# A second buffer for the rank rows of the gated layer, and an earlier place for one split

## The chip, the cores and the metric

The kernel runs on one core of a Trainium2 chip. The metric is the device time of one launch in microseconds (us), as the median of several runs. Five engines work side by side, each through its own list of instructions in order: TensorE (PE, matmuls), ScalarE (ACT), VectorE (DVE), GpSimd (POOL) and SyncE (SP), which here issues nearly all transfers. They meet by semaphores: an instruction adds to one when it is done, another engine waits until the count is reached. SBUF is the on-chip memory of 128 partitions; PSUM is the matmul output, eight banks of 128x512 floats.

## The reference

The input x is 8 batches of 128 tokens by 512. Four layers follow, each added to x: a matmul with an adapter's weight (layer 0), a dense layer with gated low-rank experts (layer 1), a dense layer with bias and low-rank part (layer 2), and the gated layer with low-rank parts (layer 3):

```
gate = x @ W_gate.T + SCALE * (x @ A_gate[id].T) @ B_gate[id].T
up   = x @ W_up.T   + SCALE * (x @ A_up[id].T)   @ B_up[id].T
act  = silu(gate) * up                      # 1376 columns, here 11 chunks of 128
x    = x + act @ W_down.T + SCALE * (act @ A_down[id].T) @ B_down[id].T
```

Each batch has its own adapter id. The change lies in the gate and up part of layer 3. B_gate and B_up, the "rank rows", are 16 rows for each batch and chunk.

## The kernel before

The product with W_gate and W_up is made in 11 steps (`STEPS`). Steps 2p and 2p+1 are pair p: two chunks of the 1376 columns, step 2p for gate and 2p+1 for up; the last step (n = 10) takes the one odd chunk with gate and up in it. In a step the two chunks, the two halves of the 512 inputs and the two halves of the tokens form a 2x2 block product, done with seven half-size products in place of eight (Winograd's scheme). So a step has seven `product` calls on PE (L1342, six matmuls each at L1347 to L1349): p1, p2, then `lora_w` (L1370), p5, p6, p3, `lora_y`, p7, p4, `lora_z_x` (L1418). The `lora` calls (L1329) add the low-rank parts, two matmuls for each of four blocks. Steps alternate between PSUM banks 0 to 3 and 4 to 7.

Every float32 operand of a matmul is split in two parts of fewer bits. For a weight tile this is a copy on ACT ("high") and a subtraction on DVE ("low"):

- `wc_high(n, part)` L618 and `wc_low(n, part)` L967 split the weights of step n in three parts: 0 (the blocks of p1 and p2), 1 (the four sums S1 to S4 that POOL forms in `form_s(n)`, L506) and 2 (the block of p4). p1(n) waits for the first, p5(n) for the second, p4(n) for the third. `form_s(n)` waits for `wc_low(n-1, 1)`, since s_tmp has one buffer.
- `bgu_high(n, i)` L629 and `bgu_low(n, i)` L972 split the rank rows of step n, chunk i (128x512). `lora_w(n)` waits for i = 0, `lora_z_x(n)` for i = 1. `bgu_high(n, i)` waits for the rows to have landed and for `c22_ready`, that is for `lora_z_x(n-2)` to be done with the place it writes.

The partial sums go from PSUM to `part` by `copy_part(n, k)` on ACT (L673, k = 0 to 3, after p1, p5, p6, p7); PE's p6 waits for k = 0, p3 for k = 1, p7 for k = 2, and the second half of `lora_z_x` for k = 3. `add_c(n, k)` on DVE (L1033) adds the bank to it after the `lora` call k. For a gate step `silu(p, k)` on ACT (L681) waits for `add_c(2p, k)`; `act_product(p, k)` on DVE (L1041) multiplies it with the up step's sum into `act_f`, which holds chunk fc in 4 KB per partition from 24 KB of the region `act` on. For n >= 2 the orders of ACT and DVE are a loop (L740, L1108) that interleaves the splits for step n+1 with the copies and sums of step n; `silu(p, 0)` and `silu(p, 1)` stand just ahead of `copy_part(2p, 3)`, and `bgu_high(n+1, i)` behind it. Steps 0 and 1 and the splits for step 2 are written out by hand.

Transfers are issued by SP in one list. `load_bgu(p)` (L432) brings the rank rows of pair p (eight transfers of 128 KB, one per batch) into the one buffer `bgu_raw`. It may write only when the rows of the pair before are split:

```
for p in range(1, PAIRS + 1):
    sp.wait_ge(bgu_ready, bgu_count(2 * p - 1, 1))
    load_bgu(p)
    if p < PAIRS:
        sp.wait_ge(wc_lo, 3 * 2 * p)
        for fc in F_ORDER[2 * p + 2:2 * p + 4]:
            load_wgu(fc)
```

`load_wgu` brings the weights of one chunk (512 KB), for the pair after the next. The last semaphore named in the change, `main_done`, counts the output tiles of layers 1 and 2; at 16 all of layer 2's matmuls are done, and with them the last readers of what lay at 44 to 52 KB of `act`.

Of the kernel before, what the change touches and what calls it, by code (L numbers as in the profile page):

```python
# [35 lines left out]
P = 128  # L36
B, S, D = 8, 128, 512
# [20 lines left out]
STEPS = 2 * PAIRS + 1  # L58
# [3 lines left out]
def bass_four_residual_layers(nc, xT, ids0, ids1, ids2, ids3, w0, w1, aw1, b1, w2, a2, b2, bias2,  # L62
                              wgu, agu, sel, bgu, wd, ad, bd, out):
    ctx = ExitStack()
    with ctx:
# [14 lines left out]
        o_slot2 = o_raw + 16 * KB  # L80
# [33 lines left out]
        t3_sb = at("t3_sb", o_w0, [H, S])  # L114
        t3_sel = at("t3_sel", o_act + 68 * KB, [2, 2, P])
        t3_st = at("t3_st", o_tp, [2, T], F32R)
        bgu_raw = at("bgu_raw", o_slot2, [2, B // 2, 2, P])
        bgu_st = [at(f"bgu_st{i}", o_bst + i * 4 * KB, [B // 2, 2, P], F32R) for i in range(2)]
        wgu_raw = [at(f"wgu_raw{i}", o_raw + i * 4 * KB, [C, 2, P]) for i in range(4)]
        xt = [at(f"xt{i}", o_xa + i * 8 * KB, [2, 2, HT], F32R) for i in range(3)]  # L120
# [56 lines left out]
        def sem(name):  # L177
            return ctx.enter_context(nc.semaphore(name))
# [7 lines left out]
        w2_in, a2_in, b2_in, bias_in = sem("w2_in"), sem("a2_in"), sem("b2_in"), sem("bias_in")  # L186
        agu_in, sel_in = sem("agu_in"), sem("sel_in")
        wgu_in = [sem(f"wgu_in{i}") for i in range(4)]
        bgu_in = sem("bgu_in")
        ad_in, bd_in = sem("ad_in"), sem("bd_in")  # L190
        wd_in = [sem(f"wd_in{o}") for o in range(C)]
        out_sent = sem("out_sent")
# [135 lines left out]
        def wgu_block(n, i, first, end):  # L328

            fc, g = rows_of(n)[i]  # L330
            return wgu_raw[raw_slot(fc)][:, first:end, g]

        def bgu_views(n, i):

            raw = bgu_raw[:, 0, :, i] if n == STEPS - 1 else bgu_raw[:, i, :, n % 2]
            return raw, bgu_st[1 - i][:, :, n % 2]

        def bgu_count(n, i):
# [41 lines left out]
        def _(sp):  # L380
# [50 lines left out]

            def load_bgu(p):  # L432

                for b in range(B):
                    rows = slice(64 * (b % 2), 64 * (b % 2) + 64)
                    if p < PAIRS:
                        f1 = 2 * p + 1
                        sp.dma_start(bgu_raw[rows, :, b // 2],  # L438
                                     bgu[adapter3[b], f1:f1 + 2].rearrange("f r n -> r f n")).then_inc(bgu_in, 16)
                    else:  # L440
                        sp.dma_start(bgu_raw[rows, 0, b // 2], bgu[adapter3[b], 0]).then_inc(bgu_in, 16)

            sp.wait_ge(w12_lo, nth["w2_3"])
            load_wgu(1)
# [4 lines left out]
            sp.wait_ge(l2_tm, 2)  # L449
            for b in range(B):  # L450
                sp.dma_start(ad_raw[:, b], ad[adapter3[b]]).then_inc(ad_in, 16)
            for p in range(1, PAIRS + 1):
                sp.wait_ge(bgu_ready, bgu_count(2 * p - 1, 1))
                load_bgu(p)
                if p < PAIRS:
                    sp.wait_ge(wc_lo, 3 * 2 * p)
                    for fc in F_ORDER[2 * p + 2:2 * p + 4]:
                        load_wgu(fc)
# [71 lines left out]
        def _(act):  # L530
# [87 lines left out]
            def wc_high(n, part_of):  # L618
                src, hi, _ = wc_views(n, part_of)
                if part_of == 0:  # L620
                    if n >= 2:
                        act.wait_ge(c21_ready, n - 1)
                    for fc, _ in rows_of(n):
                        act.wait_ge(wgu_in[raw_slot(fc)], 16 * raw_uses(fc))
                elif part_of == 1:
                    act.wait_ge(s_formed, 4 * (n + 1))
                high(hi, src).then_inc(wc_hi, 1)

            def bgu_high(n, i):  # L629
                raw, st = bgu_views(n, i)  # L630
                act.wait_ge(bgu_in, 16 * B * (n // 2 + 1))
                if n >= 2:
                    act.wait_ge(c22_ready, n - 1)
                elif i == 1:
                    act.wait_ge(main_done, 16)
                high(st, raw).then_inc(bgu_hi, 1)
# [36 lines left out]
            def copy_part(n, k):  # L673

                done, b = ((p1_done, 0), (p5_done, 2), (p6_done, 0), (p7_done, 0))[k]
                act.wait_ge(done, n + 1)
                if n >= 2:
                    act.wait_ge(silu_done if n % 2 == 0 else act_mul, 4 * (n // 2))
                high(part[n % 2][k][:], bank[4 * (n % 2) + b][:]).then_inc(part_copied[n % 2], 1)
# [49 lines left out]
            for k in (0, 1):  # L729
                silu(0, k)  # L730
            wc_high(2, 0)
            copy_part(1, 3)
            for k in (2, 3):
                silu(0, k)
            for part_of in (1, 2):
                wc_high(2, part_of)
            for i in range(2):
                bgu_high(2, i)

            for n in range(2, STEPS):  # L740
                p, g = divmod(n, 2)
# [45 lines left out]
        def _(dve):  # L787
# [253 lines left out]
            def act_product(p, k):  # L1041
                i, h = c_place(k)
                dst = act_f[:, rows_of(2 * p)[i][0], h * HT:(h + 1) * HT]
                dve.wait_ge(silu_done, 4 * p + k + 1)
                dve.wait_ge(c_added, 8 * p + 4 + k + 1)
                dve.tensor_tensor(dst, part[1][C_PART[k]][:], dst, ALU.mult).then_inc(act_mul, 1)
# [51 lines left out]
            wc_low(2, 0)  # L1098
            add_c(1, 0)
            act_product(0, 0)  # L1100
            for part_of in (1, 2):
                wc_low(2, part_of)
            add_c(1, 1)
            act_product(0, 1)
            for i in range(2):
                bgu_low(2, i)

            for n in range(2, STEPS):  # L1108
                p, g = divmod(n, 2)
# [496 lines left out]
```

## Time and profile before

| | |
|---|---|
| median of 3 runs | 301.67 us (300.73 to 302.11) |
| the profiled execution, its own time | 303.5 us |
| its span, first to last instruction | 301.7 us |
| mean granted TensorE clock | 0.987 of full |
| busy: PE, DVE, ACT, POOL | 291.2, 197.8, 143.8, 45.9 us |
| chain that ended last, by engine | PE 80%, DVE 7%, DMA 5%, ACT 3% |

The span is what lies between the first and the last instruction of the trace; the execution's own time holds 1.8 us more around it. All times of rows below are in microseconds from the span's start. A timeline row gives the start of the first instruction of a group, the time from there to the end of the last, and in brackets how long the engine sat idle before it and who released it. Consecutive matmuls overlap: the distance of two starts is what one costs.

### The profile page before, as it was taken

The page shows a single profiled execution, that of the slowest core. Times are in us where ns is not written, and L with a number is a line of the kernel's source. Part 1 is how long each engine was busy: PE and PEld are TensorE (multiplying, and loading weights), DVE is VectorE, ACT ScalarE, POOL GpSimd, SP SyncE. Part 2 cuts the span into 40 slices and gives each one's busy share as a digit, 9 for nine tenths or more (in the row PEclk, how much of TensorE's full clock was granted, in tenths as well). Part 3 has the DMA queues.
Part 4 walks back from the last instruction along what each step waited for, and adds up shares of the span by engine and source line. Part 5 has one row for each costly group of instructions (what it writes and reads, how often), then busy time and mean ns, then how long its engine had stood idle before and what let it go on. Part 6 is the DMA issues. An engine that isn't in the chain of part 4 may idle for free.

```text
span 301.7 us, 4571 instructions
## 1 busy us (share of the span) xinstructions
PE 291.2 (96%) x1624; PEld 239.0 (79%) x1624; DVE 197.8 (66%) x343; ACT 143.8 (48%) x255; POOL 45.9 (15%) x67
## 2 busy tenths in 40 slices
PE   6999999999999999959999999999999999999995
PEld 5457788988888788847888888888889888888884
DVE  1288897985567999776686786776656959242003
ACT  2378672503335297834646636656634874211000
POOL 1000000001706207043053043123000000000000
PEclk9999999999999999987999999999999999999999
DMA  4999863008403000250250350420275200022005
GB/s 153 351 393 395 323 236 107 0 4 259 156 0 99 0 3 0 88 193 0 79 199 2 107 174 0 128 84 8 63 276 180 73 0 0 0 72 70 0 2 139
DMA packets 23255, 33.29 MB, mean 110 GB/s; under 512 B 2624, under 2 KB 15424, under 8 KB 23104
## 3 DMA queue, kind: packets, MB, share of 16 engines
q1 hardware_dynamic: 22944, 32.47, 32.2%
q10 hardware_dynamic: 288, 0.52, 0.5%
q8 instruction: 13, 0.21, 0.3%
q14 instruction: 10, 0.08, 0.1%
HBM read 30.89 MB, written 2.10 MB: 109 GB/s over the span
## 4 chain that ended last, share of the span: by engine, by line
PE 80%; DVE 7%; DMA 5%; ACT 3%; SPq 2%; issue 2%
PE bank L1224 11%; PE bank L1225 11%; PE bank L1226 11%; PE bank L1347 10%; PE bank L1348 10%; PE bank L1349 10%; DMA w_raw<-in_w 4%; PE bank L1329 3%; PE bank L1179 2%; PE bank L1197 2%; PE bank L1472 2%; SPq L438 2%; DMA bgu_raw<-in_bgu 1%; DVE bgu_st L964 1%; PE bank L1208 1%
## 5 line engine op out<-in xcount | busy, mean ns | idle before, releaser
L533 ACT ACTIVATE part<-bank 128x512 f32<-128x512 f32 x44 | 26.2, 595 | 33.0 <-PE bank L1349 33.0
L1224 PE MATMUL bank<-act_hl,wd_hl 128*128 128x512 f32 (+1 forms) x99 | 36.5, 369 | 0.0
L1225 PE MATMUL bank<-act_hl,wd_hl 128*128 128x512 f32 (+1 forms) x99 | 36.3, 367 | 0.0
L1226 PE MATMUL bank<-act_hl,wd_hl 128*128 128x512 f32 (+1 forms) x99 | 36.2, 366 | 0.0
L1039 DVE TENSOR_TENSOR part<-bank,part 128x512 f32<-128x512 f32 x44 | 29.1, 682 | 6.8 <-PE bank L1329 6.8
L964 DVE SCALAR_TENSOR_TENSOR bgu_st<-bgu_st,lo_rows,bgu_raw 128x512 fp32r<-128x512 f32 x22 | 17.8, 845 | 12.6 <-ACT bgu_st L533 12.5
L790 DVE TENSOR_TENSOR w_hl<-w_raw,w_hl 128x512 fp32r<-128x512 f32 x29 | 19.0, 686 | 9.0 <-ACT w_hl L533 9.0
L533 ACT ACTIVATE act_hl<-act_f 128x512 fp32r<-128x512 f32 x22 | 13.6, 625 | 20.8 <-PE bank L1226 18.8
L790 DVE TENSOR_TENSOR act_hl<-act_f,act_hl 128x512 fp32r<-128x512 f32 x22 | 14.9, 689 | 12.9 <-ACT act_hl L533 12.8
L533 ACT ACTIVATE w_hl<-w_raw 128x512 fp32r<-128x512 f32 x29 | 17.7, 624 | 9.0 <-DMA w_raw<-in_w 8.6
L515 POOL TENSOR_TENSOR s_tmp<-wgu_raw 128x256 f32<-128x256 f32 x11 | 8.4, 760 | 86.8 <-DVE wc_up L790 42.8
L1226 PEld LDWEIGHTS bank<-act_hl,wd_hl 128*128 128x128 f32 x99 | 18.6, 188 | 3.1
L1224 PEld LDWEIGHTS bank<-act_hl,wd_hl 128*128 128x128 f32 x99 | 18.7, 189 | 3.0 <-issue 0.2
L1225 PEld LDWEIGHTS bank<-act_hl,wd_hl 128*128 128x128 f32 x99 | 18.7, 189 | 2.7
L1329 PEld LDWEIGHTS bank<-t_st,bgu_st 128*128 128x128 f32 x88 | 14.8, 191 | 6.4 <-DVE bgu_st L964 3.7
L1347 PE MATMUL bank<-xb,wc_gate 128*128 128x512 f32 x48 | 19.6, 409 | 0.0
L1329 PE MATMUL bank<-t_st,bgu_st 128*128 128x256 f32 x88 | 16.2, 289 | 3.3 <-DVE bgu_st L964 3.3
L1349 PE MATMUL bank<-xb,wc_gate 128*128 128x512 f32 x48 | 19.4, 403 | 0.0
L1348 PE MATMUL bank<-xb,wc_gate 128*128 128x512 f32 x48 | 19.3, 403 | 0.0
L685 ACT ACTIVATE act_f<-part 128x512 f32<-128x512 f32 x22 | 13.6, 630 | 10.8 <-DVE part L1039 10.8
L1081 DVE TENSOR_TENSOR x_f<-bank,x_f 128x512 f32<-128x512 f32 (+1 forms) x9 | 5.5, 629 | 19.5 <-PE bank L1493 19.5
L1347 PE MATMUL bank<-xb,wc_up 128*128 128x512 f32 x40 | 15.8, 395 | 0.0
(162 smaller groups left out, 702.5 us busy)
## 6 DMA issues: line engine op xcount, KB each, us to landing
w_raw<-in_w SPq DMA_DIRECT2D x22, 256.0 KB, 7.6
wgu_raw<-in_wgu SPq DMA_DIRECT2D x11, 512.0 KB, 4.4
bgu_raw<-in_bgu SPq DMA_DIRECT2D x40, 128.0 KB, 2.7
w_raw<-in_w SPq DMA_DIRECT2D x7, 512.0 KB, 7.4
wd_raw<-in_wd SPq DMA_DIRECT2D x4, 704.0 KB, 6.1
out<-x_f SPq DMA_DIRECT2D x7, 256.0 KB, 2.4
x_f<-in_xT SPq DMA_DIRECT2D x6, 256.0 KB, 8.2
w_raw<-in_w SPq DMA_DIRECT2D x1, 1024.0 KB, 5.7
```

What stands on the lines that cost most here:

```text
L533: return act.activation(dst, src, ACT.Copy)
L685: act.activation(act_f[:, fc, h * HT:(h + 1) * HT], part[0][C_PART[k]][:], ACT.Silu).then_inc(silu_done, 1)
L790: return dve.tensor_tensor(dst, src, hi.bitcast(F32), ALU.subtract)
L964: return dve.scalar_tensor_tensor(out=st, in0=st.bitcast(F32), scalar=lo_rows16[:, 0:1], in1=raw, op0=ALU.mult, op1=ALU.add)
L1039: dve.tensor_tensor(dst[:], bank[4 * (n % 2) + b][:], dst[:], ALU.add).then_inc(c_added, 1)
L1224: pe.matmul(dst, w_hi, x[0][:, cols], start=start, stop=False)
L1225: pe.matmul(dst, w_hi, x[1][:, cols], start=False, stop=False)
L1226: return pe.matmul(dst, w_lo, x[0][:, cols], start=False, stop=stop)
L1329: ins = pe.matmul(dst[:, q * 2 * S:(q + 1) * 2 * S], bgu_views(n, i)[1][:, pair], t3_st[:, g, pair * 2 * S:(pair + 1) * 2 * S], start=Fals ...
L1347: pe.matmul(dst[:], hi, x[0][c], start=(start and c == 0), stop=False, skip_group_check=True)
L1348: pe.matmul(dst[:], hi, x[1][c], start=False, stop=False, skip_group_check=True)
L1349: ins = pe.matmul(dst[:], lo, x[0][c], start=False, stop=(stop and c == 1), skip_group_check=True)
```

## The change

The rank rows of pair 1 (steps 2 and 3) get a buffer and a semaphore of their own, at 44 to 52 KB of `act`, where `act_f` keeps chunks 5 and 6, first written in step 4. All other pairs use the old buffer. SP issues the load of pair 1 once `main_done` has reached 16, right behind the loads of `ad`; in the loop it still waits for `bgu_ready` at p = 1, but then goes on to the weights. The splits of step 2's rank rows move: on ACT `bgu_high(2, i)` from behind `wc_high(2, 2)` to behind `wc_high(2, 0)`, and on DVE `bgu_low(2, i)` from behind `act_product(0, 1)` to ahead of `wc_low(2, 1)`.

```
--- before.py
+++ after.py
@@ -114,7 +114,7 @@
         t3_sb = at("t3_sb", o_w0, [H, S])
         t3_sel = at("t3_sel", o_act + 68 * KB, [2, 2, P])
         t3_st = at("t3_st", o_tp, [2, T], F32R)
-        bgu_raw = at("bgu_raw", o_slot2, [2, B // 2, 2, P])
+        bgu_raw = [at(f"bgu_raw{i}", off, [2, B // 2, 2, P]) for i, off in enumerate([o_slot2, o_act + 44 * KB])]
         bgu_st = [at(f"bgu_st{i}", o_bst + i * 4 * KB, [B // 2, 2, P], F32R) for i in range(2)]
         wgu_raw = [at(f"wgu_raw{i}", o_raw + i * 4 * KB, [C, 2, P]) for i in range(4)]
         xt = [at(f"xt{i}", o_xa + i * 8 * KB, [2, 2, HT], F32R) for i in range(3)]
@@ -186,7 +186,7 @@
         w2_in, a2_in, b2_in, bias_in = sem("w2_in"), sem("a2_in"), sem("b2_in"), sem("bias_in")
         agu_in, sel_in = sem("agu_in"), sem("sel_in")
         wgu_in = [sem(f"wgu_in{i}") for i in range(4)]
-        bgu_in = sem("bgu_in")
+        bgu_in = [sem(f"bgu_in{i}") for i in range(2)]
         ad_in, bd_in = sem("ad_in"), sem("bd_in")
         wd_in = [sem(f"wd_in{o}") for o in range(C)]
         out_sent = sem("out_sent")
@@ -330,9 +330,18 @@
             fc, g = rows_of(n)[i]
             return wgu_raw[raw_slot(fc)][:, first:end, g]
 
+        def bgu_place(p):
+
+            return 1 if p == 1 else 0
+
+        def bgu_landed(p):
+
+            return 16 * B * (p if p > 1 else 1)
+
         def bgu_views(n, i):
 
-            raw = bgu_raw[:, 0, :, i] if n == STEPS - 1 else bgu_raw[:, i, :, n % 2]
+            raw = bgu_raw[bgu_place(n // 2)]
+            raw = raw[:, 0, :, i] if n == STEPS - 1 else raw[:, i, :, n % 2]
             return raw, bgu_st[1 - i][:, :, n % 2]
 
         def bgu_count(n, i):
@@ -431,14 +440,15 @@
 
             def load_bgu(p):
 
+                raw, landed = bgu_raw[bgu_place(p)], bgu_in[bgu_place(p)]
                 for b in range(B):
                     rows = slice(64 * (b % 2), 64 * (b % 2) + 64)
                     if p < PAIRS:
                         f1 = 2 * p + 1
-                        sp.dma_start(bgu_raw[rows, :, b // 2],
-                                     bgu[adapter3[b], f1:f1 + 2].rearrange("f r n -> r f n")).then_inc(bgu_in, 16)
+                        sp.dma_start(raw[rows, :, b // 2],
+                                     bgu[adapter3[b], f1:f1 + 2].rearrange("f r n -> r f n")).then_inc(landed, 16)
                     else:
-                        sp.dma_start(bgu_raw[rows, 0, b // 2], bgu[adapter3[b], 0]).then_inc(bgu_in, 16)
+                        sp.dma_start(raw[rows, 0, b // 2], bgu[adapter3[b], 0]).then_inc(landed, 16)
 
             sp.wait_ge(w12_lo, nth["w2_3"])
             load_wgu(1)
@@ -449,9 +459,12 @@
             sp.wait_ge(l2_tm, 2)
             for b in range(B):
                 sp.dma_start(ad_raw[:, b], ad[adapter3[b]]).then_inc(ad_in, 16)
+            sp.wait_ge(main_done, 16)
+            load_bgu(1)
             for p in range(1, PAIRS + 1):
                 sp.wait_ge(bgu_ready, bgu_count(2 * p - 1, 1))
-                load_bgu(p)
+                if p > 1:
+                    load_bgu(p)
                 if p < PAIRS:
                     sp.wait_ge(wc_lo, 3 * 2 * p)
                     for fc in F_ORDER[2 * p + 2:2 * p + 4]:
@@ -628,7 +641,7 @@
 
             def bgu_high(n, i):
                 raw, st = bgu_views(n, i)
-                act.wait_ge(bgu_in, 16 * B * (n // 2 + 1))
+                act.wait_ge(bgu_in[bgu_place(n // 2)], bgu_landed(n // 2))
                 if n >= 2:
                     act.wait_ge(c22_ready, n - 1)
                 elif i == 1:
@@ -729,13 +742,13 @@
             for k in (0, 1):
                 silu(0, k)
             wc_high(2, 0)
+            for i in range(2):
+                bgu_high(2, i)
             copy_part(1, 3)
             for k in (2, 3):
                 silu(0, k)
             for part_of in (1, 2):
                 wc_high(2, part_of)
-            for i in range(2):
-                bgu_high(2, i)
 
             for n in range(2, STEPS):
                 p, g = divmod(n, 2)
@@ -1098,12 +1111,12 @@
             wc_low(2, 0)
             add_c(1, 0)
             act_product(0, 0)
+            for i in range(2):
+                bgu_low(2, i)
             for part_of in (1, 2):
                 wc_low(2, part_of)
             add_c(1, 1)
             act_product(0, 1)
-            for i in range(2):
-                bgu_low(2, i)
 
             for n in range(2, STEPS):
                 p, g = divmod(n, 2)
```

## Rows read from the trace of the kernel before

**Rows 1.** Waits of the matmul engine (PE) over the whole span: total, times, longest, in us.

```profile
PE bank L1329 <- DVE bgu_st L964: 3.3, 1, 3.3
```

**Rows 2.** Timeline of PE: start us, us, engine, line, tiles, form, count, [idle before <-releaser].

```profile
6.76 5.56 PE L1197 MATMUL bank<-w_raw,x_f 128*128 128x512 f32 x8 [1.02 <-DMA w_raw<-in_w]
...
127.89 0.39 PE L1347 MATMUL bank<-xb,wc_gate 128*128 128x512 f32 x1
...
130.41 0.40 PE L1349 MATMUL bank<-xb,wc_gate 128*128 128x512 f32 x1
134.08 0.80 PE L1329 MATMUL bank<-t_st,bgu_st 128*128 128x256 f32 x2 [3.28 <-DVE bgu_st L964]
...
144.90 0.40 PE L1347 MATMUL bank<-xb,wc_up 128*128 128x512 f32 x1
...
155.43 0.39 PE L1347 MATMUL bank<-xb,wc_gate 128*128 128x512 f32 x1
```

**Rows 3.** Busy time by window: us, busy per engine (instructions), granted clock, DMA share, GB/s.

```profile
3.00:12.40 9.40, 8.38 (x22) 4.76 (x22) 0.56 (x1) 0.77 (x2) 0.00 (x0) 1.00 0.80 258
102.40:113.00 10.60, 10.60 (x105) 8.54 (x105) 9.69 (x13) 8.00 (x17) 0.00 (x0) 1.00 0.01 2
130.60:134.10 3.50, 0.22 (x2) 0.02 (x1) 1.95 (x3) 1.49 (x3) 2.47 (x3) 0.91 0.77 287
134.10:140.20 6.10, 6.10 (x15) 4.87 (x16) 5.34 (x8) 2.37 (x5) 0.00 (x0) 0.50 0.02 6
144.90:155.60 10.70, 10.70 (x53) 9.00 (x52) 7.97 (x12) 6.37 (x12) 3.09 (x4) 1.00 0.51 167
```

**Rows 4.** Timeline of SyncE's DMA queue, 90 to 160 us.

```profile
90.53 4.32 SPq L451 DMA_DIRECT2D ad_raw<-in_ad  x8
122.81 6.13 SPq L438 DMA_DIRECT2D bgu_raw<-in_bgu  x8
128.98 1.07 SPq L430 DMA_DIRECT2D wgu_raw<-in_wgu  x2
145.98 6.07 SPq L438 DMA_DIRECT2D bgu_raw<-in_bgu  x8
```

**Rows 5.** Timeline of ScalarE (ACT), 90 to 160 us.

```profile
123.81 0.62 ACT L533 ACTIVATE wc_gate<-wgu_raw 128x512 fp32r<-128x512 f32 x1
125.76 0.60 ACT L533 ACTIVATE part<-bank 128x512 f32<-128x512 f32 x1 [1.33 <-PE bank L1349]
...
132.61 1.15 ACT L533 ACTIVATE bgu_st<-bgu_raw 128x512 fp32r<-128x512 f32 x2 [3.97 <-DMA bgu_raw<-in_bgu]
...
143.25 0.60 ACT L533 ACTIVATE part<-bank 128x512 f32<-128x512 f32 x1
...
148.10 0.58 ACT L533 ACTIVATE part<-bank 128x512 f32<-128x512 f32 x1
...
154.35 1.15 ACT L533 ACTIVATE bgu_st<-bgu_raw 128x512 fp32r<-128x512 f32 x2
```

**Rows 6.** Timeline of VectorE (DVE), 90 to 160 us.

```profile
126.79 0.69 DVE L1046 TENSOR_TENSOR act_f<-part,act_f 128x512 f32<-128x512 f32 x1
128.38 1.23 DVE L790 TENSOR_TENSOR wc_gate<-s_tmp,wc_gate 128x1024 fp32r<-128x1024 f32 x1 [0.89 <-ACT wc_gate L533]
...
129.85 0.68 DVE L1039 TENSOR_TENSOR part<-bank,part 128x512 f32<-128x512 f32 x1
130.64 1.12 DVE L1046 TENSOR_TENSOR act_f<-part,act_f 128x512 f32<-128x512 f32 x1
133.28 1.42 DVE L964 SCALAR_TENSOR_TENSOR bgu_st<-bgu_st,lo_rows,bgu_raw 128x512 fp32r<-128x512 f32 x2 [1.51 <-ACT bgu_st L533]
134.61 1.28 DVE L1039 TENSOR_TENSOR part<-bank,part 128x512 f32<-128x512 f32 x2
...
137.61 0.68 DVE L1039 TENSOR_TENSOR part<-bank,part 128x512 f32<-128x512 f32 x1
```

**Rows 7.** Timeline of GpSimd (POOL), 90 to 150 us.

```profile
129.77 0.77 POOL L515 TENSOR_TENSOR s_tmp<-wgu_raw 128x256 f32<-128x256 f32 x1 [8.92 <-DVE wc_gate L790]
```

More of the change, by code:

```diff
@@ L116, in bass_four_residual_layers @@
         t3_st = at("t3_st", o_tp, [2, T], F32R)
-        bgu_raw = at("bgu_raw", o_slot2, [2, B // 2, 2, P])
+        bgu_raw = [at(f"bgu_raw{i}", off, [2, B // 2, 2, P]) for i, off in enumerate([o_slot2, o_act + 44 * KB])]
         bgu_st = [at(f"bgu_st{i}", o_bst + i * 4 * KB, [B // 2, 2, P], F32R) for i in range(2)]
@@ L188, in bass_four_residual_layers @@
         wgu_in = [sem(f"wgu_in{i}") for i in range(4)]
-        bgu_in = sem("bgu_in")
+        bgu_in = [sem(f"bgu_in{i}") for i in range(2)]
         ad_in, bd_in = sem("ad_in"), sem("bd_in")
@@ L331, in wgu_block, with bgu_place, bgu_landed @@
             return wgu_raw[raw_slot(fc)][:, first:end, g]
+        def bgu_place(p):
+            return 1 if p == 1 else 0
+        def bgu_landed(p):
+            return 16 * B * (p if p > 1 else 1)
         def bgu_views(n, i):
-            raw = bgu_raw[:, 0, :, i] if n == STEPS - 1 else bgu_raw[:, i, :, n % 2]
+            raw = bgu_raw[bgu_place(n // 2)]
+            raw = raw[:, 0, :, i] if n == STEPS - 1 else raw[:, i, :, n % 2]
             return raw, bgu_st[1 - i][:, :, n % 2]
@@ L432, in load_bgu @@
             def load_bgu(p):
+                raw, landed = bgu_raw[bgu_place(p)], bgu_in[bgu_place(p)]
                 for b in range(B):
@@ L437, in load_bgu @@
                         f1 = 2 * p + 1
-                        sp.dma_start(bgu_raw[rows, :, b // 2],
-                                     bgu[adapter3[b], f1:f1 + 2].rearrange("f r n -> r f n")).then_inc(bgu_in, 16)
+                        sp.dma_start(raw[rows, :, b // 2],
+                                     bgu[adapter3[b], f1:f1 + 2].rearrange("f r n -> r f n")).then_inc(landed, 16)
                     else:
-                        sp.dma_start(bgu_raw[rows, 0, b // 2], bgu[adapter3[b], 0]).then_inc(bgu_in, 16)
+                        sp.dma_start(raw[rows, 0, b // 2], bgu[adapter3[b], 0]).then_inc(landed, 16)
             sp.wait_ge(w12_lo, nth["w2_3"])
@@ L451, in _ @@
                 sp.dma_start(ad_raw[:, b], ad[adapter3[b]]).then_inc(ad_in, 16)
+            sp.wait_ge(main_done, 16)
+            load_bgu(1)
             for p in range(1, PAIRS + 1):
                 sp.wait_ge(bgu_ready, bgu_count(2 * p - 1, 1))
-                load_bgu(p)
+                if p > 1:
+                    load_bgu(p)
                 if p < PAIRS:
@@ L630, in bgu_high @@
                 raw, st = bgu_views(n, i)
-                act.wait_ge(bgu_in, 16 * B * (n // 2 + 1))
+                act.wait_ge(bgu_in[bgu_place(n // 2)], bgu_landed(n // 2))
                 if n >= 2:
@@ L731, in _ @@
             wc_high(2, 0)
+            for i in range(2):
+                bgu_high(2, i)
             copy_part(1, 3)
@@ L736, in _ @@
                 wc_high(2, part_of)
-            for i in range(2):
-                bgu_high(2, i)
             for n in range(2, STEPS):
@@ L1100, in _ @@
             act_product(0, 0)
+            for i in range(2):
+                bgu_low(2, i)
             for part_of in (1, 2):
@@ L1104, in _ @@
             act_product(0, 1)
-            for i in range(2):
-                bgu_low(2, i)
             for n in range(2, STEPS):
```

## The prediction

> **What bounds the kernel now.** I read the waits of PE first, since PE is busy nearly the whole span. They show one wait worth naming after the start: 3.3 us, once, for the split rank rows [rows 1]. The timeline of PE places it: p2 of step 2 issues its last matmul at 130.41, and the next instruction, `lora_w(2)`, starts at 134.08 after 3.28 us of idle [rows 2]. Matmuls go out every 0.23 us (127.89 to 130.41 is 2.52 for 11 of them), so `lora_w(2)` could have started at 130.64: 3.44 us lost. The windows show a second loss: behind the gap, from 134.1 to 140.2, the granted clock is 0.50, the 1.2 GHz level, where the step after has 1.00, 2.4 GHz [rows 3]. PE had stood still before it fell, and worked without a break when it rose.
>
> Both losses are read from step lengths. Step 2 takes 144.90 - 127.89 = 17.01 us, step 3 takes 155.43 - 144.90 = 10.53 [rows 2]. The excess is 6.48 us: 3.44 of gap and 3.04 of half clock. That is the most that removing this wait can bring.
>
> Who makes the wait? ACT sat 3.97 us until the rows had landed at 132.61, split them and let DVE go at 133.28 [rows 5, 6]. SP had issued the eight transfers from 122.81 to 128.94 [rows 4], because their one buffer came free only with the splits of step 1. So the chain is: split of step 1, eight issues, landing, ACT, DVE, PE. In later pairs the same chain starts at the same place but has a whole step to run in, and PE does not wait.
>
> **The load of pair 1.** It moves from 122.81 to the end of layer 2's matmuls, about 102.5. SP's queue is empty then: its transfers before ended at 94.85 [rows 4]. From first issue to ACT's start the load took 132.61 - 122.81 = 9.8 us, so it lands near 112.3. ACT will ask for it at 124.3: 12 us of cover, and the bound of this cost from above is what would be left if the load took twice as long, still nothing. Behind it on SP stands the wait for `bgu_ready` that was there before (it let SP go at 122.81), and behind that two weight loads, which now go out at 122.8 instead of 128.98; their readers are in step 4, after 140, so that earlier place brings nothing. Could the eight transfers disturb work at 102.4 to 113, where PE is busy 10.60 of 10.60 and DVE 9.69 [rows 3]? Nothing shows them there. The nearest row is the window 144.9 to 155.6, with a DMA share of 0.51, clock 1.00 and PE without idle time [rows 3]. I take 0. The far end of the bound: a DVE subtraction or product goes from 0.69 to 1.12 in the worst neighbourhood of the trace, beside POOL [rows 6, 7]; if all of DVE's 9.69 us stretched like that it would cost 6 us. I give it little weight, since DVE's sums last 0.68 both at 129.85, with transfers under way, and at 137.61, with a DMA share of 0.02, and a product with both inputs in SBUF 0.69 at 126.79, beside the transfers [rows 3, 6].
>
> **ACT's order.** The two copies of `bgu_high(2)` (1.15 us) now follow `wc_high(2, 0)`, which starts at 123.81 and lasts 0.62, so they run 124.3 to 125.5. `copy_part(1, 3)` is behind them; it starts at 125.76 when PE lets it, after 1.33 us of idle [rows 5]. The copies fit in that idle: cost 0. Were they 0.5 us longer, `copy_part(1, 3)` would still be ready long before PE needs it at 127.4 or so. Its condition, the end of `lora_z_x(0)`, lies 18 matmuls and eight `lora` matmuls of 0.12 ahead of p1(2), so at 127.89 - 5.1 = 122.8, in time.
>
> **DVE's order.** Here cover is thin. `bgu_low(2)` now starts when `act_product(0, 0)` has issued, at 127.40 (126.79 + 0.6), and takes 134.61 - 133.28 = 1.33 [rows 6]. So `wc_low(2, 1)` starts at 128.73 instead of 128.38 and ends near 129.95. p5(2) asks for it at 130.64 + 0.24 = 130.88: 0.9 us of slack. `lora_w(2)` finds its rows from 128.2 on. The gap at 130.64 goes, and with it the fall of the clock.
>
> What is late next is DVE. Before, it caught up while PE stood and while PE ran at half clock. Now it has this list from 128.73 on, with durations from [rows 6]: `wc_low(2, 1)`, `wc_low(2, 2)` and `add_c(1, 1)` 2.26 (128.38 to 130.64), so to 130.99; `act_product(0, 1)` 1.12 beside POOL, to 132.1; two sums, a split, two products and the sum `add_c(2, 0)`, before from 134.61 to 138.29, of which the next can start at 3.6, to 135.7; `wc_low(3, 1)` and `(3, 2)` 1.47 (128.38 to 129.85), to 137.2; `add_c(2, 1)` 0.68, to 137.85. Then ACT's `silu(1, 1)` 0.63 and `copy_part(2, 3)` 0.60, with 0.04 of handing over each, to 139.15. Only then may the second half of `lora_z_x(2)` go. PE, at full rate from 127.89, is there at 127.89 + 10.53 - 0.24 = 138.2. **So a new wait of 0.9 us** arises at the end of step 2.
>
> It has a small echo. Before, from the start of `copy_part(2, 3)` at 143.25 to the end of `copy_part(3, 0)` at 148.68 it took 5.43 us [rows 5], through the splits, DVE's sums and two silus. From 138.55 on that ends at 144.0. PE wants it for p6(3) at 139.15 + 0.24 + 18 x 0.23 + 0.24 = 143.8: 0.2 us more. After that step 3 stands as before against the other engines.
>
> The load of pair 2 starts when `bgu_low(3)` is done, in which step 3 is now about 0.8 us later against PE. ACT took its rows at 154.35 [rows 5]; from ACT's start to the first split ready it is 133.28 + 0.75 - 132.61 = 1.4 [rows 5, 6], so they were ready near 155.8. `lora_w(4)` needed them 12 matmuls after 155.43, near 158.2. Of 2.4 us of slack about 1.6 are left. Cost 0.
>
> **Sum.** 3.44 + 3.04 - 0.9 - 0.2 = 5.4 us, of which I take 5.3 (a semaphore or two more in a chain of so many steps). The profiled execution has 303.5 us, its span 301.7; it would be 298.2. The median of the runs shown lies 1.8 lower, at 301.67, and I carry the same difference over: **296.4 us**. The bounds of the new waits: none if DVE's product is not stretched and its order closes up; 2 us if every sum and split in the list stretches as the product did for the 3.4 us in which POOL forms its sums. So the case runs from 295.2 to 297.4.
>
> **Rivals.** What this kernel's measurement can tell from no change is 0.5%, 1.5 us.
>
> 1. No new wait at all: 6.48 us gained, 295.2. For it: ACT and DVE are idle in part of each steady step (DVE 7.97 of 10.70, [rows 3]). Against: the list above has no gap in it.
> 2. The new wait brings the clock down once. 0.50 for 6.1 us cost 3.04, so the gain is 5.4 - 3.0 = 2.4 and the time 299.3. For: the clock fell once after an idle time. Against: PE sat idle 1.02 us until 6.76, and the window around it, 3.0 to 12.4, has clock 1.00 [rows 2, 3]. 0.9 is nearer to 1.02 than to 3.28.
> 3. Slower: the clock falls again and again, at the short waits that ends of steps now have while DVE is behind. The place is the end of steps 2, 3, 4; each fall costs 3.0. It decides once 6.48 + 1.5 = 8.0 us are lost, that is 1.1 of waits and 2.3 falls; three falls give 301.67 - 6.48 + 1.1 + 9.1 = 305.4. Against: at half clock PE is slow enough for DVE to catch up (step 2 of before), so one fall ends the cause. The Trainium skill's page "TensorE: Matmul & The Clock Gate", in "A second HAM failure mode: psum-queue depth-cycling", says that short idle times between groups of matmuls, frequent enough, make the clock swing between its two levels. By that rule this rival is what would come; the trace so far has only the 1.02 us at full clock against it.
> 4. The change doesn't bring what it says: pair 1's load is held up beyond 130, or its transfers stretch the stretch from 102 to 113 by the 6 us of the bound above. Then 301.7. Against it stand 12 us of cover and the equal durations beside DMA.
>
> **How the numbers follow.** The forecast gets 0.62, rival 1 0.17, rival 2 0.12, rival 4 0.05, rival 3 0.04. The range runs from 294.8 (rival 1 and half a us for medians of runs that spread over 1.4) to 299.6, which takes in rival 2 and leaves out 3 and 4. Faster is the sum of the first three, 0.91; within 0.5% 0.05; slower 0.04.
>
> **What would show it.** The waits of PE name no `bgu_st` of 3 us. The granted clock stays 1.00 from 115 on, and step 2 takes near 11.4 us from p1 to p1, step 3 near 10.7. Eight transfers of rank rows start near 102.5. A wait below 1 us stands ahead of the last `lora` matmuls of step 2, released by ACT's copy into `part`. I am wrong if the clock falls in steps 2 to 4, if `p5(2)` waits for DVE, or if PE idles between 102 and 122.

## The result, and the profile after

The changed kernel takes 298.67 us (median of 6 runs, 298.31 to 299.24) against 301.63 us for the kernel before (6 runs): ratio 0.9921, interval 0.9897 to 0.9945. That is 0.8% faster, 2.4 us by the ratio (the two medians differ by 3.0 us), where 5.3 us were forecast. The direction and the range held; the size was about twice what came.

The changed kernel was compared once more on another chip, after the first experiments below, with a ratio of 0.990 to 0.993 expected and a mean clock of 0.998 or more in nearly all of its runs; had a part of the gain belonged to the first chip, the ratio would have been nearer to 0.995. It came to 298.98 us against 301.33 us, ratio 0.9921 (0.9892 to 0.9950), with 0.999 or 1.00 in five of six runs and 0.994 in one.

The profiled execution shows a span of 296.7 us and a clock of 1.00. Against the profiled execution of before (301.7) that is 5.0 us less, very near the forecast. So the first question is why the profiles differ by 5.0 us and the runs by less than 3.

The waits of PE after the start, in answer to [rows 1]: the 3.3 us for `bgu_st` are gone, and two short ones for ACT's copies into `part` have come.

```profile
PE bank L1342 <- ACT part L546: 0.7, 1, 0.7
...
PE bank L1360 <- ACT part L546: 0.2, 1, 0.2
```

The timeline of PE, in answer to [rows 2]:

```profile
127.77 0.39 PE L1360 MATMUL bank<-xb,wc_gate 128*128 128x512 f32 x1
...
130.51 0.40 PE L1342 MATMUL bank<-t_st,bgu_st 128*128 128x256 f32 x2
...
139.04 0.51 PE L1342 MATMUL bank<-t_st,bgu_st 128*128 128x256 f32 x2 [0.73 <-ACT part L546]
139.38 0.40 PE L1360 MATMUL bank<-xb,wc_up 128*128 128x512 f32 x1
...
144.16 0.50 PE L1360 MATMUL bank<-xt,wc_up 128*128 128x512 f32 x1 [0.25 <-ACT part L546]
...
150.47 0.39 PE L1360 MATMUL bank<-xb,wc_gate 128*128 128x512 f32 x1
```

`lora_w(2)` follows p2 at once, at 130.51. Step 2 lasts 139.38 - 127.77 = 11.61 us, step 3 lasts 150.47 - 139.38 = 11.09. The wait at the end of step 2 and its echo at p6(3) stand where the forecast put them, with 0.73 and 0.25 us for 0.9 and 0.2.

Three windows, in answer to [rows 3] (columns as there). The clock is 1.00 in all of them. In the first, with the rank rows now coming in, DVE is busy 9.84 us and was 9.69, and PE has no idle time:

```profile
102.40:113.00 10.60, 10.60 (x105) 8.53 (x99) 9.84 (x13) 8.01 (x17) 0.00 (x0) 1.00 0.33 101
...
127.00:139.00 12.00, 11.31 (x54) 9.27 (x53) 10.73 (x16) 6.86 (x13) 5.27 (x7) 1.00 0.01 1
139.00:150.00 11.00, 10.71 (x49) 8.63 (x50) 7.86 (x11) 6.54 (x12) 3.81 (x6) 1.00 0.42 124
```

SyncE's queue, in answer to [rows 4]: the load of pair 1 starts at 102.50, the weights at 122.51, pair 2's rows at 141.41.

```profile
102.50 6.13 SPq L448 DMA_DIRECT2D bgu_raw<-in_bgu  x8
122.51 0.82 SPq L439 DMA_DIRECT2D wgu_raw<-in_wgu  x2
141.41 6.08 SPq L448 DMA_DIRECT2D bgu_raw<-in_bgu  x8
```

ACT, in answer to [rows 5]: the two copies of rank rows run at 124.18, `copy_part(1, 3)` still has 0.32 us of idle ahead of it. `wc_high(3, 1)` waits 0.51 for POOL; `silu(1, 1)` and `copy_part(2, 3)` are the end of the chain that holds PE.

```profile
124.18 1.14 ACT L546 ACTIVATE bgu_st<-bgu_raw 128x512 fp32r<-128x512 f32 x2
125.63 0.60 ACT L546 ACTIVATE part<-bank 128x512 f32<-128x512 f32 x1 [0.32 <-PE bank L1362]
...
133.45 1.06 ACT L546 ACTIVATE wc_up<-s_tmp 128x1024 fp32r<-128x1024 f32 x1 [0.51 <-POOL s_tmp L533]
...
137.87 0.63 ACT L698 ACTIVATE act_f<-part 128x512 f32<-128x512 f32 x1 [1.44 <-DVE part L1052]
138.41 0.58 ACT L546 ACTIVATE part<-bank 128x512 f32<-128x512 f32 x1
```

DVE, in answer to [rows 6]: from 127.27 to 137.84 (137.16 + 0.68) it is never idle. The product beside POOL takes 1.13 and the split at 133.12 takes 0.85 instead of 0.68.

```profile
127.27 1.41 DVE L977 SCALAR_TENSOR_TENSOR bgu_st<-bgu_st,lo_rows,bgu_raw 128x512 fp32r<-128x512 f32 x2
128.60 1.22 DVE L803 TENSOR_TENSOR wc_gate<-s_tmp,wc_gate 128x1024 fp32r<-128x1024 f32 x1
...
130.86 1.13 DVE L1059 TENSOR_TENSOR act_f<-part,act_f 128x512 f32<-128x512 f32 x1
...
133.12 0.85 DVE L803 TENSOR_TENSOR wc_up<-wgu_raw,wc_up 128x512 fp32r<-128x512 f32 x1
133.89 1.28 DVE L1059 TENSOR_TENSOR act_f<-part,act_f 128x512 f32<-128x512 f32 x2
...
137.16 0.68 DVE L1052 TENSOR_TENSOR part<-bank,part 128x512 f32<-128x512 f32 x1
139.54 1.70 DVE L977 SCALAR_TENSOR_TENSOR bgu_st<-bgu_st,lo_rows,bgu_raw 128x512 fp32r<-128x512 f32 x2 [1.71 <-ACT bgu_st L546]
```

### The profile page after: what moved, and what is told of

Read it like the earlier page. It is cut to its first block, busy times and chain, and to the rows that moved or that the text cites. A ratio compares the mean times of both kernels' runs of the same rounds, so it can differ in the third digit from the quotient of the medians.

```text
span 296.7 us, 4572 instructions
## 1 busy us (share of the span) xinstructions
PE 286.5 (97%) x1624; PEld 235.8 (79%) x1624; DVE 197.0 (66%) x343; ACT 143.8 (48%) x255; POOL 45.3 (15%) x67
## 4 chain that ended last, share of the span: by engine, by line
PE 86%; DVE 5%; DMA 4%; issue 2%; ACT 1%; SPq 1%; DVEq 0%; ACTq 0%
PE bank L1237 12%; PE bank L1238 12%; PE bank L1239 12%; PE bank L1360 10%; PE bank L1361 10%; PE bank L1362 10%; DMA w_raw<-in_w 4%; PE bank L1342 3%; PE bank L1192 2%; PE bank L1485 2%; PE bank L1221 1%; PE bank L1284 1%; PE bank L1174 1%; PE bank L1222 1%; PE bank L1223 1%
## 5 line engine op out<-in xcount | busy, mean ns | idle before, releaser
L1360 PE MATMUL bank<-xb,wc_gate 128*128 128x512 f32 x48 | 18.9, 394 | 0.0
L1362 PE MATMUL bank<-xb,wc_gate 128*128 128x512 f32 x48 | 18.9, 394 | 0.0
L1361 PE MATMUL bank<-xb,wc_gate 128*128 128x512 f32 x48 | 18.8, 392 | 0.0
```

Of the source, the lines that this page charges most:

```text
L1360: pe.matmul(dst[:], hi, x[0][c], start=(start and c == 0), stop=False, skip_group_check=True)
L1361: pe.matmul(dst[:], hi, x[1][c], start=False, stop=False, skip_group_check=True)
L1362: ins = pe.matmul(dst[:], lo, x[0][c], start=False, stop=(stop and c == 1), skip_group_check=True)
```

## Why the runs gained less than the profiles: the kernel before, again

These runs take the kernel before again, and then the two halves of the change by themselves.

**The unchanged kernel.** No edit.

> The unchanged kernel once more, for the spread of its own runs. Theory T1: the term of the forecast that was mis-sized is the half clock behind the gap. The profiled execution of before took 303.5 us with 3.04 us lost to the clock; the median run takes 301.6, 1.9 less, so most runs should lose only about 1.1 us to the clock, and their mean granted clock should lie above 0.987, near 0.993 to 0.996. Rival T2: the clock loses 3 us in every run and the 1.9 us lie in the loads at the start, which differ between executions; then the clocks of all runs are near 0.987 and the spans differ without it. A gap of 3.4 us is there in every profile under both.

Measured: 301.14 us (12 runs), ratio 1.0007. In this profile the span is 299.1 and the clock 1.00. DVE and PE:

```profile
131.12 1.12 DVE L1046 TENSOR_TENSOR act_f<-part,act_f 128x512 f32<-128x512 f32 x1
132.16 2.36 DVE L964 SCALAR_TENSOR_TENSOR bgu_st<-bgu_st,lo_rows,bgu_raw 128x512 fp32r<-128x512 f32 x2
```

```profile
133.43 0.51 PE L1329 MATMUL bank<-t_st,bgu_st 128*128 128x256 f32 x2 [2.15 <-DVE bgu_st L964]
...
146.54 0.50 PE L1347 MATMUL bank<-xt,wc_up 128*128 128x512 f32 x1 [0.29 <-ACT part L533]
```

Here the rows were taken by ACT at 131.41, 8.15 us after the first issue at 123.26, not after 9.8. DVE went from `act_product(0, 1)` to `bgu_low(2)` without idle. So the gap of 2.15 us was set by DVE's list, and the clock did not fall. Two more profiles of the same kernel were taken at the end, on a third chip:

> A third profile of the unchanged kernel, to see the usual execution. If DVE's list sets the gap in most executions, the rows land 8.0 to 8.7 us after the first issue, the gap is 2.1 to 2.3 us, and where the mean clock is below 1.00 its fall stands directly behind the gap, in 131 to 141, and costs 0.5 to 1.5 us. If the first profile was the usual one, the gap is above 3 us again.

> A fourth profile of the unchanged kernel; the same is expected of it as of the third.

In the third profile (301.05 us) the rows are taken after 8.13 us and the gap is 2.16 us, as in the second. But here the clock fell behind the gap, to 0.50 from 133.8 to 137.2, and it took PE 6.05 us from `lora_w(2)` to `lora_y(2)`, where the second profile has 4.46 (133.43 to 137.89):

```profile
132.97 0.50 PE L1329 MATMUL bank<-t_st,bgu_st 128*128 128x256 f32 x2 [2.16 <-DVE bgu_st L964]
...
139.02 0.39 PE L1329 MATMUL bank<-t_st,bgu_st 128*128 128x256 f32 x2
```

The fourth profile (302.78 us) is like the first in the landing: ACT waits 4.00 us for rows that it takes 9.84 us after their first issue at 123.35, and PE's gap is 3.32 us.

```profile
133.19 1.15 ACT L533 ACTIVATE bgu_st<-bgu_raw 128x512 fp32r<-128x512 f32 x2 [4.00 <-DMA bgu_raw<-in_bgu]
```

Expectation and outcome agree for the third and not for the fourth. In both profiles with late rows it is the last of the eight transfers alone that is late: it lands 4.2 and 4.3 us after its issue, where the seven others take 2.6 to 2.9 us, and the last one takes 2.6 us in the second and the third profile.

The four profiles of before, with the time from `lora_w(2)` to `lora_y(2)`, in which the clock is lowered or not, and with the stretch from the last `lora` matmuls of step 1 to those of step 3 (in the first profile 127.42 to 154.96):

| execution | rows taken after | gap | mean clock | `lora_w(2)` to `lora_y(2)` | stretch |
|---|---|---|---|---|---|
| before, the first, on which the forecast rests | 9.80 us | 3.28 us | 0.987 | 7.34 us | 27.54 us |
| the second | 8.15 | 2.15 | 1.00 | 4.46 | 24.48 |
| the third | 8.13 | 2.16 | 0.992 | 6.05 | 25.10 |
| the fourth | 9.84 | 3.32 | 0.994 | 6.05 | 26.30 |
| the changed kernel, two profiles | | 0.73 at the end of step 2 | 1.00 | 4.38 | 22.70 and 22.71 |

What is left of the span outside the stretch is nearly the same in all six, 274.0 to 274.7 us, so the difference of the two kernels lies in the stretch. The first profile has the longest stretch and the lowest clock: its clock is at 0.50 from about 133.5 to about 140.3, for 6.8 us, against 3.4 us in the third and in the fourth (135.4 to 138.8). The fall costs PE 2.9 us in the first (7.34 against 4.46) and 1.6 us in the third and the fourth. Of the 1.6 us only 0.6 show in the stretch at the gap of 2.15 us (25.10 against 24.48). The other 1.0 stands in the second profile as waits of PE for what DVE's list makes late: the last `lora` matmuls of step 2 take 0.4 us more there, and p6(3), with the 0.29 us shown above, loses 0.6. Behind a slow PE both are gone. At the gap of 3.3 us DVE has caught up already and the whole 1.6 us show.

Of 58 runs of before with a recorded clock (12 of them from the repetition above, the others from the comparisons on two chips), 19 have a mean clock of 1.00 and a median time of 300.71 us, 29 lie at 0.992 or 0.994, and 10 below 0.99, from 301.74 to 303.54 us. The profiled execution of 303.5 us belongs to the last. (One more run of before, on the third chip, took 299.72 us at a clock of 0.994.) Only 8 of the 58 took more than 302.4 us, as both profiles with late rows did. A run without a profile shows no landing, so this is an estimate from times: late rows are nearer to one execution in seven than to the one in two of the profiles.

Theory T1 was half right: most runs lose less to the clock. But landing and gap vary as well, which it had denied, and T2, differences in the loads at the start, isn't needed. With the third profile as the usual one (its 301.05 us are near the median of the 58 runs, 301.2) the change is worth 25.10 - 22.70 = 2.4 us, which is what the ratio of 0.9921 says.

**The early load alone.** From the changed kernel, the two moves of splits are undone:

```
             wc_high(2, 0)
-            for i in range(2):
-                bgu_high(2, i)
             copy_part(1, 3)
...
             for part_of in (1, 2):
                 wc_high(2, part_of)
+            for i in range(2):
+                bgu_high(2, i)
...
             act_product(0, 0)
-            for i in range(2):
-                bgu_low(2, i)
...
             act_product(0, 1)
+            for i in range(2):
+                bgu_low(2, i)
```

> Pair 1's rows loaded early to their own place, the splits of step 2 in the order of before. The copies on ACT then run at about 128.6, the two on DVE behind act_product(0, 1) at about 131.7, the first ready near 132.5, where lora_w(2) asks at 130.6: a gap of 1.8 to 2.0 us in place of 3.4. Under T1 and T2 alike the wait is this long. If a gap of 1.9 us keeps the clock at 1.00 then DVE has 1.9 us more to catch up and the wait at the end of step 2 goes: about 0.9 to 1.0 us over the changed kernel, 299.5. If the clock falls as well, up to 3 us more.

Measured: 301.02 us (12 runs), ratio 1.000 (0.9981 to 1.0019). The gap is 2.15 us. ACT has the copies made at 128.96, two microseconds ahead of need:

```profile
128.96 1.14 ACT L546 ACTIVATE bgu_st<-bgu_raw 128x512 fp32r<-128x512 f32 x2
```

but DVE comes to them only behind the product:

```profile
131.05 1.13 DVE L1059 TENSOR_TENSOR act_f<-part,act_f 128x512 f32<-128x512 f32 x1
132.11 2.34 DVE L977 SCALAR_TENSOR_TENSOR bgu_st<-bgu_st,lo_rows,bgu_raw 128x512 fp32r<-128x512 f32 x2
```

The gap is 2.15 us where 1.8 to 2.0 were expected, with the pair of splits at 2.34 us beside POOL. The expected 299.5 us was 1.5 too low: I had let one wait of about 1 us stand for the whole, but the gap, 0.4 us at the last `lora` matmuls of step 2 and an echo of 0.28 us in step 3 all stay, so the stretch is 24.47 us against 22.70; and the clock was lowered in 7 of the 12 runs. What the run shows is that the new buffer alone brings nothing that can be measured, to within 0.6 us. A late landing cost 1.2 us (26.30 against 25.10) and can't reach PE here; had it been there in half of the executions of before, this run should have been about 0.6 us faster, which is the edge of its interval. A second profile:

> A second profile of the early load alone. The landing can't reach PE here, so the gap is 2.1 to 2.2 us again whatever the execution. If the mean clock is below 1.00, the fall stands behind the gap, which would show that a gap of 2.15 us is enough for it in some executions, without any late landing.

The gap is 2.15 us again, and this time the clock fell behind it, with the landing out of the question:

```profile
100.00:130.00 30.00, 30.00 (x201) 24.48 (x200) 26.75 (x35) 21.65 (x39) 6.79 (x7) 1.00 0.21 71
...
133.00:136.00 3.00, 2.24 (x9) 1.90 (x10) 3.00 (x5) 0.00 (x0) 1.22 (x2) 0.84 0.02 5
136.00:139.00 3.00, 3.00 (x10) 2.36 (x9) 3.00 (x6) 1.92 (x3) 0.00 (x0) 0.59 0.00 0
139.00:142.00 3.00, 3.00 (x16) 2.50 (x15) 1.68 (x3) 2.06 (x5) 2.23 (x3) 1.00 0.00 0
```

Between 133 and 139 the granted clock is 0.84 and 0.59, from 100 to 133 and behind 139 it is 1.00. One and the same gap of 2.15 us left the clock alone in the first profile and not in the second. The stretch grew from 24.47 to 25.10 us, 0.6 us for the fall and not 3.0. As in the kernel before, the fall is shorter than the one that I read (1.6 us of PE's time), and while PE is slow, DVE catches up: the echo of 0.28 us and the 0.4 us at the end of step 2 are gone. The mean clock of this profile, 0.987, holds a second fall, from 12 to 16 us, where the granted clock is 0.57; so a mean clock alone does not say where the clock fell.

**The new order alone**, with the load as before (the same moves of ACT and DVE, in the kernel before):

> The splits of step 2 at their new place, the load as before. ACT then waits for rows that land near 132.5 with copy_part(1, 3), two silus and the second part of the weights behind it, so PE waits at lora_z_x(1), at 127.4, for copy_part(1, 3) until about 134.3, and then for p5(2)'s weights. Expected 5 to 8 us slower than before, 306 to 310, with the clock at its lower level behind it. If it is not slower than 303 I have the chain of ACT wrong.

Measured: 305.66 us, ratio 1.0151 (1.0123 to 1.0179). ACT stands 7.06 us until the rows land, with `copy_part(1, 3)` behind it, and PE waits 5.33 us for that copy:

```profile
131.72 1.15 ACT L533 ACTIVATE bgu_st<-bgu_raw 128x512 fp32r<-128x512 f32 x2 [7.06 <-DMA bgu_raw<-in_bgu]
132.77 0.58 ACT L533 ACTIVATE part<-bank 128x512 f32<-128x512 f32 x1
```

```profile
133.40 0.79 PE L1329 MATMUL bank<-t_st,bgu_st 128*128 128x256 f32 x2 [5.33 <-ACT part L533]
```

The chain is as expected, and so is the clock, 0.50 from 130 to 136; the time is 0.3 us below the lower end. The two halves are worth 0.0 and +4.6 us alone and -2.4 together: the order needs the load, and the load shows no gain without the order.

## DVE's list, tested

**Products later.** The changed kernel, DVE's list in step 2:

```
-                if g == 0:
+                if g == 0 and n != 2:
                     for k in (2, 3):
                         act_product(p - 1, k)
...
                 add_c(n, 1)
+                if n == 2:
+                    for k in (2, 3):
+                        act_product(0, k)
```

> The changed kernel with act_product(0, 2) and (0, 3) moved from ahead of add_c(2, 0) to behind add_c(2, 1) on DVE: 1.2 us less ahead of add_c(2, 1). If DVE's list in step 2 is what makes PE wait 0.7 us at the end of step 2 and 0.25 us in step 3, both waits go and the time falls by 0.7 to 1.0 us below the changed kernel, to about 297.8. Rival: it is POOL's sums, 0.2 us later than before, that hold wc_high(3, 1) and all behind it; then the wait stays above 0.4.

Measured: 298.27 us, ratio 0.9908 (0.9885 to 0.9931). The time alone doesn't tell it from the changed kernel (0.9897 to 0.9945); the trace does. The wait at the end of step 2 is gone, though ACT's `wc_high(3, 1)` still waits 0.51 us for POOL, so it was DVE's list and not POOL's sums. But the echo in step 3 grew from 0.25 to 0.76 us:

```profile
143.76 0.50 PE L1363 MATMUL bank<-xt,wc_up 128*128 128x512 f32 x1 [0.76 <-ACT part L546]
```

```profile
136.11 0.68 DVE L1052 TENSOR_TENSOR part<-bank,part 128x512 f32<-128x512 f32 x1
136.71 1.83 DVE L1059 TENSOR_TENSOR act_f<-part,act_f 128x512 f32<-128x512 f32 x2
138.50 2.34 DVE L977 SCALAR_TENSOR_TENSOR bgu_st<-bgu_st,lo_rows,bgu_raw 128x512 fp32r<-128x512 f32 x2
```

The two products moved to 136.71, beside POOL's sums for step 4, and took 1.83 us in place of 1.28; the two splits behind them took 2.34 in place of 1.70. Half of the expected gain was eaten there: the stretch is 22.26 us, 0.44 below the changed kernel.

**Splits ahead of the product.** The early load alone, with one more edit in DVE's list:

```
             add_c(1, 1)
+            for i in range(2):
+                bgu_low(2, i)
             act_product(0, 1)
-            for i in range(2):
-                bgu_low(2, i)
```

> Pair 1's rows early, ACT's order of before, and on DVE bgu_low(2) ahead of act_product(0, 1) instead of behind it. If DVE's list, not the landing, sets the gap of 2.15 us, then it starts about 1.05 us earlier (131.0 instead of 132.1) and the gap is 1.0 to 1.5 us. The rest of DVE's list is as long as before, so up to 0.5 us of it comes back as a wait at the end of step 2. Time 300.2 to 300.7, 0.3 to 0.8 us below the early load alone. If the gap stays at 2.1, POOL's sums beside bgu_low, not the order, hold it.

Measured: 299.68 us (12 runs), ratio 0.9941 (0.9922 to 0.9959), 0.5 us better than the range.

```profile
130.83 0.50 PE L1342 MATMUL bank<-t_st,bgu_st 128*128 128x256 f32 x2 [0.45 <-DVE bgu_st L977]
...
139.93 0.50 PE L1342 MATMUL bank<-t_st,bgu_st 128*128 128x256 f32 x2 [1.24 <-ACT part L546]
...
145.05 0.50 PE L1360 MATMUL bank<-xt,wc_up 128*128 128x512 f32 x1 [0.25 <-ACT part L546]
```

The gap fell from 2.15 to 0.45 us. I had expected 1.0 to 1.5, with the splits held by POOL; but the first split got in between POOL's first and second sum and it was the second sum that stretched, to 1.29 us from 0.72, and the pair took 1.88 us instead of 2.34. 1.24 us came back at the end of step 2. This is the list at work: what is taken from the first wait comes back in part at the next.

The stretch is 23.88 us, 0.59 below the early load alone, within the 0.3 to 0.8 expected. The runs gained more, 1.3 us by the medians and 1.8 by the ratios. A part of that is likely the clock, though no profile shows it: 11 of these 12 runs have a mean clock of 0.997 or more, where the early load alone has 5 of 12 at 1.00.

**DVE's new order without ACT's:**

```
             wc_high(2, 0)
-            for i in range(2):
-                bgu_high(2, i)
             copy_part(1, 3)
...
             for part_of in (1, 2):
                 wc_high(2, part_of)
+            for i in range(2):
+                bgu_high(2, i)
```

> Pair 1's rows early and DVE's new order, but ACT's order of before. bgu_high(2) then runs at 128.9 to 130.1, bgu_low(2) from 129.5 to 130.9, and wc_low(2, 1) behind it to 132.1, so lora_w(2) waits little and p5(2) waits about 1.2 us; DVE's list is 2 us later than in the changed kernel, so the wait at the end of step 2 is 1.5 to 2 us. Time 300.5 to 301.5, no better than before. If it comes to 298.7, ACT's new order is worth nothing and DVE's is all.

Measured: 300.57 us (10 runs), ratio 0.9984 (0.9960 to 1.0009), within the expectation. DVE waits for ACT's copies at 128.50, and everything behind is late. PE has four short waits:

```profile
131.10 0.50 PE L1360 MATMUL bank<-xb,wc_gate 128*128 128x512 f32 x1 [0.77 <-DVE wc_gate L803]
...
136.27 0.50 PE L1360 MATMUL bank<-xt,wc_gate 128*128 128x512 f32 x1 [0.54 <-ACT part L546]
...
140.27 0.50 PE L1342 MATMUL bank<-t_st,bgu_st 128*128 128x256 f32 x2 [0.73 <-ACT part L546]
...
145.40 0.50 PE L1360 MATMUL bank<-xt,wc_up 128*128 128x512 f32 x1 [0.28 <-ACT part L546]
```

The wait at p5(2) is 0.77 instead of 1.2, and at the end of step 2 0.73 instead of 1.5 to 2, since 0.54 of it is spent at p7(2) already. The stretch is 24.52 us, as long as with the early load alone (24.47). So ACT's move carries weight, 1.6 us by the medians on this chip (300.57 against 298.98), though it stood in the forecast at a cost of 0 and no gain. The profiled execution was the fastest of the ten and has a clock of 1.00; four of the ten have 0.993 or 0.994 and took 301.39 to 301.74 us. No profile shows where the clock fell in those.

**Rows early.** The changed kernel with both waits attacked. On ACT `bgu_high(3)` goes ahead of `silu(1, 1)`; on DVE `act_product(0, 2)` and `(0, 3)` go behind `add_c(2, 3)`:

```
                 elif g == 0:
-                    for k in (0, 1):
-                        silu(p, k)
+                    silu(p, 0)
+                    if n == 2:
+                        for i in range(2):
+                            bgu_high(n + 1, i)
+                    silu(p, 1)
                 copy_part(n, 3)
-                if more:
+                if more and n != 2:
...
                 for k in (2, 3):
                     add_c(n - 1, k)
+                if n == 3:
+                    for k in (2, 3):
+                        act_product(0, k)
...
-                if g == 0:
+                if g == 0 and n != 2:
                     for k in (2, 3):
                         act_product(p - 1, k)
```

> The changed kernel with three more moves around step 2: bgu_high(3) on ACT ahead of silu(1, 1), and act_product(0, 2) and (0, 3) on DVE behind add_c(1+1, 2) and (1+1, 3) in the list of step 3 instead of ahead of add_c(2, 0). This takes 1.2 us out of the list ahead of add_c(2, 1) and lets bgu_low(3) start about 1.5 us sooner, so that both short waits of the changed kernel (0.73 and 0.25 us) go. Expected 0.7 to 1.0 us below the changed kernel, about 297.8, with no wait of PE between 100 and 160. Rival: as in the run with the products later alone, one wait goes and the other grows to 0.7, and the time stays within 0.3 us of the changed kernel.

Measured: 297.31 us (5 runs), ratio 0.9866 (0.9832 to 0.9899), 1.7 us below the changed kernel on the same chip (298.98), and better than both kernels. PE has no wait between 100 and 160. `bgu_low(3)` starts at 137.28 instead of 139.54:

```profile
136.68 0.69 DVE L1055 TENSOR_TENSOR part<-bank,part 128x512 f32<-128x512 f32 x1
137.28 1.89 DVE L980 SCALAR_TENSOR_TENSOR bgu_st<-bgu_st,lo_rows,bgu_raw 128x512 fp32r<-128x512 f32 x2
139.10 1.27 DVE L1055 TENSOR_TENSOR part<-bank,part 128x512 f32<-128x512 f32 x2
140.30 1.45 DVE L1062 TENSOR_TENSOR act_f<-part,act_f 128x512 f32<-128x512 f32 x2
```

The stretch is 149.10 - 127.96 = 21.14 us, so the changed kernel's 22.70 hold 1.56 us of loss, of which the trace lists 0.98 as idle. The other 0.6 us stand where matmuls start again behind a wait: the last `lora` matmuls start at 139.04 where they could have at 138.15 or so, 0.9 us for a listed 0.73, and the next product follows them after 0.34 instead of 0.23. The expectation of 0.7 to 1.0 us missed that. (The expectation's `add_c(1+1, 2)` is `add_c(2, 2)`.)

## Why the prediction was right in its steps and wrong in its size

- **Excess of step 2, 3.44 + 3.04 us: the step that failed.** Both terms were read rightly from one execution and taken for the usual one. The gap was 3.3 us in two profiles of before and 2.15 us in the two others, and by the times of the runs the shorter one is the usual. A lowered clock is usual too (39 of 58 runs have a mean clock below 1.00), but it cost 1.6 us and not 3.04 in the three other profiles that have it behind this gap (two of before, one of the early load alone), and only 0.6 net at the gap of 2.15 us. Against the usual stretch of 25.10 us the excess over the 21.14 us of the run without any wait (rows early) is 4.0 us, not 6.48.
- **"The median of the runs shown lies 1.8 lower, and I carry the same difference over."** This was where the error could have been seen. A profiled execution 1.8 us above the median, with a clock of 0.987, and a change that removes the only fall of the clock in it: the 1.8 us most likely lie in that very place, and are not to be subtracted twice. The profiles bear it out: outside the stretch the span differs by 0.7 us at most. 296.4 + 1.8 = 298.2 would have been near the measured 298.67, with some luck, since the new wait was under-sized (below).
- **"Who makes the wait?"** I named one chain, the load's, and gave DVE's other work no end of its own. `act_product(0, 1)` ended at 131.76 [rows 6], so with rows already there DVE could not have begun before about 131.7, and would then have been beside POOL. Two chains ended near 132 and 133.3; the early load cut one, the new order the other, and where the rows land early, as in the second and the third profile, only DVE's mattered.
- **The load of pair 1** went out at 102.50 (102.5 foretold) and disturbed nothing: PE idles nowhere between 102 and 122, and DVE's sums and products keep their durations.
- **ACT's order at 0, DVE's at 0.9 us of slack:** both held; p5(2) does not wait.
- **The new wait, 0.9 + 0.2 us: the second term mis-sized.** Measured 0.73 + 0.25 as idle and 1.56 as loss, 0.5 more than the 1.1 in the sum. The list itself was right: it gave 137.85 for the end of `add_c(2, 1)`, and that came at 137.84 with p1 starting 0.12 us earlier. With both terms as measured the sum is 4.0 - 1.56 = 2.4 us.
- **Two ends of ranges** are 0.2 and 0.1 us off their own terms: new waits of 2 us give 297.2 where 297.4 stands, unless the echo comes on top, and 295.2 less half a us is 294.7, not 294.8. Nothing hangs on either.
- **Rival 1**, no new wait, did not come. **Rival 2 and 3**, the clock brought down by the short waits, did not come: both profiles of the changed kernel have 1.00, and 11 of its 12 runs 0.998 or more (one has 0.994). The Trainium skill's page "TensorE: Matmul & The Clock Gate", in "A second HAM failure mode: psum-queue depth-cycling", has a clock that swings when short idle times come often enough; two of 0.73 and 0.25 us were not that. Four in the run with DVE's new order alone left its profile at 1.00 as well, but four of its ten runs lie at 0.993 or 0.994, so that by that rule such waits may bring the clock down in some executions; the runs here neither show nor exclude it.
- **Rival 4** did not come: the load was not held up and stretched nothing. The early load alone did measure 1.000, but since DVE's list kept the gap at 2.15 us, which no rival had named.

## What to carry to other kernels

When a profiled execution lies clearly above the median of its kernel, ask first whether the excess sits in the stall that the change removes; then the gain is to be counted against a second profile, not against this one. When a wait is to be removed, find for each engine on its path when it would have been ready without the thing waited for: the later of these times is all that one edit can reach. And work that an engine did while another one stood still does not vanish; write its list down behind the old wait, as it says where the next one arises.

## What the runs showed that I had not expected

The same gap of 2.15 us, in the same place of the same kernel, let the granted clock fall in one execution and not in the next (early load alone), and of its 12 timed runs 5 had a mean clock of 1.00 and 7 had 0.986 to 0.994. Not every such reading lies behind the gap: in the second profile of the early load alone the clock is also 0.57 from 12 to 16 us, and in the one profile of the last kernel above it is 0.86 in the first 12 us and 1.00 behind the place of the old gap.

Of eight transfers issued in the same 6.1 us the last one took 2.6, 2.6, 4.2 and 4.3 us from its issue to its landing in the four profiles of before, and 3.1 us in that of the new order alone, where ACT took the rows after 8.67 us. What decides was not found. Two weight transfers of 512 KB go out right behind it, and whether they hold it up was not tested.

A pair of splits on DVE took 1.41 us alone and 1.70 us with POOL at work for a part of it. Beside POOL's sums throughout it took 2.34 us, or 1.88 where its first split came in between POOL's first and second sum and the second sum was stretched instead. Sums with one input in PSUM kept 1.28 for two. The Trainium skill's page "SBUF — State Buffer", in "Who interferes with whom", says that a DVE instruction with two SBUF inputs contends with a GpSimd instruction that reads SBUF, and that one with at most one SBUF input does not, outside the modes in which DVE uses two ports. By that rule the splits are the ones to stretch and the sums are not; the traces agree with it. PE needs only the first split of the pair: it was released 1.27 us after the pair's start in the second profile of before (132.16 to 133.43), where the pair was stretched, and 0.80 us after it in the first, where it was not (133.28 to 134.08). So about 0.5 us of the gap of 2.15 us is this stretch.
